# Experts of a GNN kernel: which engine waits for the row additions of the early tiles

## The reference, cut to what matters

```python
gate_scores = x @ Wg + bg
_, idx = jax.lax.top_k(gate_scores, 2)
mask = jax.nn.one_hot(idx, 8).sum(axis=-2)
h = gelu(einsum('td,edh->teh', x, W1) + b1)     # D 256 -> H 512
y = einsum('teh,ehd->ted', h, W2) + b2          # H 512 -> D 256
out = einsum('ted,te->td', y, mask)             # x = x + out
```

## Time and profile before

| what | value |
|---|---|
| median of 3 runs | 1186.1 us (1182.18 to 1188.26) |
| the profiled execution, its own time | 1186.74 us |
| its span in the profile | 1185.2 us |
| TensorE busy | 1138.0 us, 96% of the span |
| VectorE, ScalarE, GpSimd busy | 48%, 31%, 14% |
| the experts' tiles in the trace | about 444 to 674 us |

### The profile page before, as it was taken

How to read it: one execution, slowest core, us unless ns; L and a number is a source line. 1 busy time by engine, 2 the same in 40 slices (tenths; PEclk the granted TensorE clock), 3 DMA queues, 4 the chain that set the end, 5 groups by cost and what they waited for, 6 DMA issues and landing times. The chain is left out here.

```text
span 1185.2 us, 22136 instructions
## 1 busy us (share of the span) xinstructions
PE 1138.0 (96%) x8024; PEld 855.3 (72%) x8024; DVE 566.8 (48%) x1540; ACT 361.6 (31%) x697; POOL 169.3 (14%) x160
## 2 busy tenths in 40 slices
PE   5989999999999998799999899999999999999998
PEld 4667777776668886688888767555566678866765
DVE  8888888834447678111111363000044455248654
ACT  5764544522211002233333333100022201044333
POOL 3300000000001456444344300000000000001000
PEclk9999999999999998899999899999999999999999
DMA  6610000047533346456664531130066445125101
GB/s 194 210 44 14 25 25 12 25 136 183 154 95 107 118 134 182 63 103 124 149 148 75 117 110 45 41 91 32 17 156 188 135 133 162 57 89 188 44 22 42
DMA packets 134097, 118.16 MB, mean 100 GB/s; under 512 B 23030, under 2 KB 122105, under 8 KB 134016
## 3 DMA queue, kind: packets, MB, share of 16 engines
q1 hardware_dynamic: 103392, 77.67, 22.9%
q0 software_dynamic: 12448, 18.95, 8.3%
q10 hardware_dynamic: 18176, 20.45, 5.0%
HBM read 67.34 MB, written 49.29 MB: 98 GB/s over the span
## 5 line engine op out<-in xcount | busy, mean ns | idle before, releaser
L1372 PE MATMUL b_pa<-adj,l_parts 128*128 (+2 forms) x980 | 141.7, 296 | 0.4 <-ACT adj L1303 0.4
L1372 PEld LDWEIGHTS b_pa<-adj,l_parts 128*128 128x128 f16 x980 | 91.2, 97 | 29.5 <-issue 0.5
L2748 PE MATMUL l_sum<-l_parts,ring 128*128 128x256 f32 x448 | 103.9, 386 | 6.0 <-DVE ring L2890 6.0
L2945 POOL DMA_INDIRECT x<-ring,l_row_i x54 | 84.3, 1561 | 113.2 <-DVE ring L2890 81.5
L1613 DVE SCALAR_TENSOR_TENSOR l_parts<-dense,scale,l_parts 128x256 f16<-128x256 f32 x48 | 23.2, 484 | 160.8 <-ACT l_parts L1604 160.7
L2748 PEld LDWEIGHTS l_sum<-l_parts,ring 128*128 128x128 f32 x448 | 84.8, 194 | 17.1 <-DVE ring L2890 6.2
L1580 PE MATMUL dense<-room,ring 128*128 128x512 f32 x200 | 93.9, 593 | 0.2 <-ACT ring L1561 0.2
L2299 PE MATMUL l_sum<-l_parts,adj 128*128 128x256 f16 x735 | 82.9, 273 | 1.2 <-DVE rows L2027 1.2
L2299 PE MATMUL l1b_sum<-l_parts,adj 128*128 128x256 f16 x735 | 82.9, 273 | 0.9 <-DVE rows L2027 0.9
L2299 PEld LDWEIGHTS l_sum<-l_parts,adj 128*128 128x128 f16 x735 | 71.2, 98 | 10.7 <-issue 2.7
L2299 PEld LDWEIGHTS l1b_sum<-l_parts,adj 128*128 128x128 f16 x735 | 71.4, 98 | 10.4 <-issue 2.4
(11 more groups left out here) (475 smaller groups left out, 1869.5 us busy)
## 6 DMA issues: line engine op xcount, KB each, us to landing
ring<-sums_and_zt SPq DMA_DIRECT2D x50, 256.0 KB, 3.4
l_expert_xr<-slots_in SPq DMA_DIRECT2D x28, 257.0 KB, 2.8
l_parts<-in_L_ffn_W SPq DMA_DIRECT2D x12, 512.0 KB, 4.7
pre<-room ACTq DMA_DIRECT2D x34, 128.0 KB, 2.0
sums_and_zt<-ring SPq DMA_DIRECT2D x10, 320.0 KB, 2.3
ring<-inv SPq DMA_DIRECT2D x50, 64.0 KB, 4.0
sums_and_zt<-room ACTq DMA_DIRECT2D x5, 640.0 KB, 3.4
adj<-xt SPq DMA_DIRECT2D x5, 640.0 KB, 4.4
```

The lines of the kernel that those rows point to most:

```text
L1372: ins = nc.tensor.matmul(pa[f][:, 0:size], parts[:, k, a, f * P:(f + 1) * P], adj[:, k, ds(r * BW, size)], start=k == 0 and a == 0, stop=k ...
L2748: ins = nc.tensor.matmul(to[t], h[:, n, t * P:(t + 1) * P], w2[:, u, n, :], start=i == 0, stop=i == HB - 1)
L2945: pool.indirect_dma_start(out=g["x1"], in_=rows, in_offset=None, compute_op=ALU.add, out_offset=bass.IndirectOffsetOnAxis(ap=at, axis=0)). ...
```

## The change

VectorE no longer calls `added` behind tile 0 and behind tile 1. GpSimd calls it instead, ahead of its own additions of tile 1 and of tile 2 (the two early tiles whose expert is another than the tile before them), in place of the waits for each t. Tiles 2 and 3 are written out on GpSimd, and its loop over pairs of tiles begins two tiles later.

```diff
         one_tile(0, 0, whole)
-        added(dve, 16)
         one_tile(1, 1, whole1)
-        added(dve, 16 * 2)
         for j in range(2, EARLY):
             one_tile(j, 0)
...
-        def add_rows(j, half):
+        def add_rows(j, half, other_expert=False):
             pool.wait_ge(s["ids_now"], j + 1)
+            if other_expert:
+                added(pool, 16 * j)
             for t in range(NT):
-                if not isinstance(j, int) or j:
+                if not other_expert and (not isinstance(j, int) or j):
                     pool.wait_ge(s[f"added{t}"], 16 * j)
                 pool.wait_ge(s["y_done"], NT * j + NT + t + 1)
                 pool.sem_inc(s["adding"], 1)
                 add(y[:, half, t, :], ids_now[:, half, t:t + 1], s[f"added{t}"])
 
         add_rows(0, 0)
-        add_rows(1, 1)
+        add_rows(1, 1, other_expert=True)
+        add_rows(2, 0, other_expert=True)
+        add_rows(3, 1)
...
-        with pool.Fori(1, pairs) as i:
+        with pool.Fori(EARLY // 2, pairs) as i:
```

## The result

| | before | changed |
|---|---|---|
| median | 1186.45 us (6 runs) | 1178.52 us (6 runs, 1176.69 to 1180.11) |
| profiled execution, its own time | 1186.74 us | 1178.69 us |
| its span | 1185.2 us | 1177.2 us |

A forecast was written before the change was run, and what follows sets the result against it. TensorE, busy 1138.0 of 1185.2 us, was taken as the bound, stalled behind VectorE's wait for a DMA landing. Idle time 6.11 plus clock 2.56 gave 8.67 us: 1178.1 for the profiled execution, 1177.4 us median, range 1174 to 1182.5.

The forecast's parts named there:

- The idle time, 6.11 us: TensorE ahead of tile 2's second product: with VectorE's wait gone, it starts at 476.61 in place of 482.72, gaining 6.11 us.
- The clock, 2.56 us: TensorE from tile 2's product to the next: without the idle stretch the clock stays up, 7.34 not 9.90 us, gaining 2.56.
- GpSimd's waits cost nothing: GpSimd ahead of tile 1's and 2's additions: taking the waits over leaves TensorE 0.5 and 1.1 us to spare.
- the forecast's own signs of being wrong: TensorE idle ahead of the product at 484 or 491 us, that product some 6 us long, or span not ending earlier.
- The row loads: Tile 4's rows, issued at 477.76, are in by 482.5 even at the longest landing, ahead of the turn at 483.5.
- The additions shutting VectorE out: Rival at tile 1: VectorE's reads wait for GpSimd's addition, TensorE 1.3 us late; gain 7.4, 1178.7 us; chance 0.03.
- The moved stall: Rival: longer landings stall TensorE one tile down; gain 5.1, 1181.0 us; chance 0.06 partial loss, 0.03 slower by over 0.5%.
- the point of no gain: Within the moved-stall rival: kernel becomes slower at landings of 8.8 us, or about 7.5 if the clock falls again.

The follow-up runs named there:

- the filled stall: Kernel before, with filler matmul products in TensorE's idle stretch, waits untouched: 24 products 1.0030, 12 products 1.0003 and 0.9990, 10 products 0.9983.
- the long delay: Changed kernel with 20 memsets on GpSimd between tile 0's landing and tile 1's first addition (delay 5.2 us): ratio 0.9994, gain 0.7 us.
- 5 memsets: Changed kernel with 5 memsets on GpSimd between tile 0's landing and tile 1's first addition (delay 1.4 us): ratio 0.9932, gain 8.1 us.
- first experiment: Kernel before with only the wait behind tile 0 moved to GpSimd, VectorE still waiting behind tile 1: ratio 1.0001.

## Why the prediction was right, point by point

- **The idle time, 6.11 us.** Right: the product came at 476.50, with 476.61 forecast. VectorE had tile 1 out at 475.77, where 476.05 had been allowed. Over four profiles with a stall, the time from the wanted to the actual start is 5.7 to 6.3 us.
- **The clock, 2.56 us.** Right in kind, shown by the filled stall and by the long delay. Its size varies between executions: 2.56, 1.76, 2.23, 2.69 and 2.80 us in the five profiles with a standstill of over 4 us. The forecast took one execution's value, which happens to be the middle one of the five. Idle time and clock together come to 8.67 us in the first profile of before and to 7.8 in the second, and 7.6 and 7.9 us were measured; that the forecast of the time, 1177.4 us, lies only 1.1 us from the median is in part luck.
- **GpSimd's waits cost nothing.** Nearly. Tile 0's second addition landed in 4.3 us (4.0 forecast) and GpSimd began 1.1 us behind it (1.0 forecast), so tile 2 was taken out at 483.62 (483.45 forecast) and TensorE had 0.2 us to spare, not 0.5. The term that was mis-sized is the landing of tile 1's second addition, for which the median of 3.8 us stood: it took 4.7, so VectorE had tile 3 out at 491.30, not 490.2, and TensorE was 0.25 us late. An idle stretch ahead of the product at 491 us was one of the forecast's own signs of being wrong; it came, but at 0.25 us and in one of two profiles. In the other that landing took 4.8 us and the product was on time, because GpSimd's chain stood 0.5 us earlier against TensorE there (the addition at 483.75 and the product wanted at 490.61, against 484.82 and 491.20): the forecast took the distance of one execution for fixed. Why those landings were long is open. The row load of tile 5 was issued at 485.43, within the landing; in the kernel before it came only at 494.20. But with 5 memsets an addition issued 0.4 us behind that load landed in 3.8 us, and the earlier trace rows has one of 5.5 us with no row load beside it.
- **The row loads.** Right: TensorE showed no wait for rows in these tiles. Tile 4's landed in 3.4 us, at 481.0, and the turn came at 483.41.
- **The rivals.** The additions shutting VectorE out: tile 1's two halves took 0.75 us, as always; the addition at 475.62 began 0.15 us before they ended, and the row numbers had been written before it, so this run hardly tested it, and the earlier trace rows remain the better row. The moved stall: it is what happens as soon as one of the waits stays (first experiment) or GpSimd's chain gets 5 us longer (last delay). The forecast put the point of no gain at landings of 7.5 to 8.8 us, each counted at two tiles; one landing of 4.3 with 5.2 of delay, counted at one tile, left 0.7 us. No way was found in which the kernel becomes slower.

## What to carry to other kernels

Put a wait for a DMA's landing on the engine whose next instruction needs it, here GpSimd, which issues the next colliding addition, not on one that other work queues behind. Waits in series hide each other: the second of these two had held nobody up in the profile, because the first did, and moving either alone was measured at 0.0 us. Price a stall of TensorE with the slow matmuls behind it (here 1.8 to 2.8 us on 4.4 to 6.1 us of idle time), and read both from more than one execution. Do the same for slack: here it hung on two times, each of which moved by 1.0 us or more from profile to profile.

## What was not expected of the hardware

- A standstill of about 6 us (5.5 to 6.1 us idle) cost 1.76 to 2.69 us in lower clock, by profile. At another place TensorE's clock fell in one of thirteen profiles and 25 matmuls took 4.56 us in place of 2.89, behind an idle stretch of 1.9 us; five other profiles have the same stretch there and the 25 matmuls in 2.89 us.
- The indirect additions landed in 3.8 to 5.0 us in the early tiles of the changed kernel (two profiles), where the median of all additions before the change was 3.8. What lengthens them was not found.
